# A four-unit attention and expert kernel: the last unit's jobs prepare the rows that the routed experts read

## The reference, cut to what matters

```
x = x + t0 * attention(q = norm(x), k, v = split(ctx), key bias and length mask)       # unit 0
x = x + t1 * (self-attention(norm(x)) + sum over the 2 best of 8 dense 256x256 experts) # unit 1
x = x + t2 * (attention(norm(x)) over ctx and own keys) @ w_proj.T + b_proj             # unit 2
y = norm(x)
o = causal self-attention(y) @ w_o                                                      # unit 3
h = norm(y + o) * g1 + b1
w = two best of softmax(h @ wg), scaled to sum 1
moe = sum over the two: (gelu(h @ w1[e] + bb1[e]) @ w2[e] + bb2[e]) * w[e]     # 256 -> 1024 -> 256
x = x + t3 * (norm(h + moe) * g2 + b2)
```

## Time and profile before

| | before |
|---|---|
| median of three runs | 2734.83 us (2731.59 to 2737.47) |
| the profiled execution | 2733.68 us, span 2732.0 us |
| TensorE busy | 2326.2 us |
| ScalarE, VectorE, GpSimd busy | 1381.1, 1705.4, 917.7 us |
| DMA | 296.34 MB, 108 GB/s in the mean |

### The profile page before, as it was taken

How to read it: one execution, slowest core, us unless ns; L and a number is a source line. 1 busy time by engine, 2 the same in 40 slices (tenths; PEclk the granted TensorE clock), 3 DMA queues, 4 the chain that set the end, 5 groups by cost and what they waited for, 6 DMA issues and landing times. The chain is left out here.

```text
span 2732.0 us, 52598 instructions
## 1 busy us (share of the span) xinstructions
PE 2326.2 (85%) x17492; PEld 1615.3 (59%) x17493; DVE 1705.4 (62%) x4564; ACT 1381.1 (51%) x2430; POOL 917.7 (34%) x1769
## 2 busy tenths in 40 slices
PE   3889899999999999999999999898337999999920
PEld 1445555455555555666566666665337999999920
DVE  4668796766776766766766667665455434344358
ACT  3779863454444447777777777676110222222211
POOL 5355322131232152233322257665001333333321
PEclk9989999999999999999999999999556999999965
DMA  7888633242332354454454446553560111111144
GB/s 227 215 210 209 150 97 78 51 96 55 81 82 76 94 126 117 118 122 117 113 126 118 104 110 140 133 129 76 204 189 12 35 36 36 35 35 34 36 148 167
DMA packets 214243, 296.34 MB, mean 108 GB/s; under 512 B 33109, under 2 KB 152703, under 8 KB 207776
## 3 DMA queue, kind: packets, MB, share of 16 engines
q1 hardware_dynamic: 183808, 253.78, 36.5%
q10 hardware_dynamic: 23328, 22.06, 2.6%
q0 software_dynamic: 6912, 17.97, 2.1%
HBM read 201.41 MB, written 93.22 MB: 108 GB/s over the span
## 5 line engine op out<-in xcount | busy, mean ns | idle before, releaser
L1112 DVE TENSOR_REDUCE mx<-s_ps 128x2 f32<-128x512 f32 (+1 forms) x1024 | 657.2, 683 | 217.5 <-PE s_ps L870 141.3
L995 ACT ACTIVATE ex<-t_ps 128x512 f32<-128x512 f32 (+1 forms) x1280 | 683.8, 577 | 191.7 <-PE t_ps L901 146.9
L901 PE MATMUL t_ps<-qs,ks 123*128 123x256 bf16 x2048 | 362.1, 278 | 10.3 <-ACT ex L995 6.5
L926 PE MATMUL pv_ps<-ex,va 128*32 128x256 f32 (+1 forms) x5120 | 324.7, 380 | 2.5 <-POOL ex L1035 2.5
L989 ACT ACTIVATE qs<-tr_ps 27x2048 bf16<-27x2048 bf16 x128 | 239.4, 1870 | 146.5 <-PE tr_ps L883 143.8
L847 PE MATMUL pre_ps<-wexp,xt 128*128 128x512 f32 x512 | 264.5, 625 | 6.8 <-DVE moe L1176 2.6
L1631 PEld LDWEIGHTS x_up_ps<-x_rows_t,x_wnow 128*128 128x128 f32 x2272 | 266.4, 193 | 5.3 <-issue 0.9
L1631 PE MATMUL x_up_ps<-x_rows_t,x_wnow 128*128 128x128 f32 x2272 | 267.0, 276 | 1.1 <-DVE x_pre L1694 0.7
L901 PEld LDWEIGHTS t_ps<-qs,ks 123*128 123x128 bf16 x2048 | 175.0, 99 | 143.4 <-ACT ex L995 66.2
L1641 PE MATMUL x_y_ps<-wdn,x_act 128*128 x1136 | 257.1, 379 | 0.7 <-DVE x_y L1702 0.7
L1661 ACT ACTIVATE x_rows_t<-x_rt_ps 128x256 f32<-128x256 f32 x72 | 27.7, 384 | 439.8 <-PE x_rt_ps L1620 439.8
(11 more groups left out here) (254 smaller groups left out, 3764.1 us busy)
## 6 DMA issues: line engine op xcount, KB each, us to landing
q_parts<-pq SPq DMA_DIRECT2D x128, 192.0 KB
qs<-q_parts SPq DMA_DIRECT2D x64, 384.0 KB, 5.0
qs<-q_parts SPq DMA_DIRECT2D x192, 128.0 KB, 5.8
k_parts<-pk SPq DMA_DIRECT2D x96, 192.0 KB
ks<-k_parts SPq DMA_DIRECT2D x96, 192.0 KB
ks<-k_parts SPq DMA_DIRECT2D x288, 64.0 KB
ks<-ctx_k_parts SPq DMA_DIRECT2D x64, 192.0 KB
ks<-ctx_k_parts SPq DMA_DIRECT2D x192, 64.0 KB
```

What stands on the lines that cost most here:

```text
L901: last = pe.matmul(dst[:, t * T:(t + 1) * T], key[0:ROWS, h, t * P:(t + 1) * P], qs[q_at][0:ROWS, h, :], start=True, stop=True)
L926: last = pe.matmul(pv_ps[i * VW:(i + 1) * VW, q0:T], val[:, t, k * QH + i, :], e, start=r == 0 and t == 0, stop=r == srcs - 1 and t == NT - 1,
L995: act.activation(ex[:, n % EXPS, 0:w], t_ps[n % 2][:, 0:w], ACT.Exp).then_inc(t_read, 1)
L1112: dve.tensor_reduce(dst, s_ps[n % S_BANKS][:, :].rearrange("p (a b) -> p a b", a=dst.shape[-1]), AX.X, ALU.max).then_inc(s_read, 1)
```

## The change

- The jobs of unit 3 get six more steps: `HNS` (moments of `h`, VectorE), `HNP` (root, GpSimd), `HNX` (scaling, VectorE), `HNG` (times `g1`, plus `b1`, GpSimd), `HT` (transposes and their copy by ScalarE) and `HG` (gate logits, copied by VectorE into a tile `gate_logits` that stays). The rows that they store are the normed ones. The loop of `route` is gone.
- All loads of the experts' weights stand after the attention phase: 16 halves of `wup` on ScalarE ahead of its exponential; `bup`, `bdn` and 8 of `wdn` on SyncE.
- `NX` goes from 5 to 7, `AHEAD_JOBS` from 6 to 8.
- Values are laid out 17 columns wide (`VW`) in SBUF; in PSUM the heads keep their distance of 32 (`VS`). Unit 2 loads the values' half of `ctx` from the input and GpSimd lays it out again, in place of `STOREV` and `LOADV`.
- In four jobs of unit 1 a clearing of key rows (`UNBIAS`, VectorE) is replaced by a transfer of a row of zeros (`bring_bias`).
- `JOBS` is written as a general expression of `BEHIND`; its list is the same as before. `KV_USERS`, `KEY_JOBS`, `CTX_JOBS` and `OTT_JOBS` index who used a buffer before; for this list they name the same jobs as the old expressions. `GATE` waits for the `FIN` of the job two back.

```diff
-VW = 32
+VW = HD + 1
+VS = 32
 UNITS = 4
-JOBS = [(u, b) for u in range(UNITS) for b in range(B)]
+BEHIND = (0, B, 2 * B, 3 * B)
+JOBS = [(u, n - BEHIND[u]) for n in range(B + BEHIND[-1]) for u in range(UNITS) if 0 <= n - BEHIND[u] < B]
 JOB = {job: j for j, job in enumerate(JOBS)}
 
-NX, NCTX, NPART, NQ, NKV, NO = 5, 2, 2, 3, 4, 3
+NX, NCTX, NPART, NQ, NKV, NO = 7, 2, 2, 3, 4, 3
...
+    "HNS": [("dve", 1.16)], "HNP": [("pool", 1.3)], "HNX": [("dve", 1.1)], "HNG": [("pool", 2.4)], "HT": [("pe", 0.44), ("act", 0.6)], "HG": [("pe", 0.45), ("dve", 0.2)],
...
-AHEAD_JOBS = 6
+AHEAD_JOBS = 8
 TOPS = 6
-PRE = ("XT", "KT", "Q", "K", "V", "GATE", "CT", "MBIAS", "EXPERT", "OTT", "PROJ")
+PRE = ("XT", "KT", "Q", "K", "V", "GATE", "CT", "MBIAS", "EXPERT", "OTT", "PROJ", "HT", "HG")
...
-    x = add("LOADX", 0, ("STOREX", u - 1, b, 0) if u else None, ("STOREX", *old, 0) if old else None)
+    x = add("LOADX", 0, ("STOREX", u - 1, b, 0) if u else None, (("STOREX" if old[0] < 3 else "PROJ"), *old, 0) if old else None)
...
-    if u == 0:
-        c = add("LOADC", 0, past("KT", NCTX), past("VC", NCTX))
-        values.append(add("VC", 0, c, *values_free(0), ("STOREV", 0, b - NKV, 0) if b >= NKV else None))
-        add("STOREV", 0, values[0])
-    if u == 2:
-        values.append(add("LOADV", 0, *values_free(0)))
+    if u in (0, 2):
+        before = CTX_JOBS[CTX_AT[(u, b)] - NCTX] if CTX_AT[(u, b)] >= NCTX else None
+        c = add("LOADC", 0, ("VC", *before, 0) if before else None, ("KT", *before, 0) if before and before[0] == 0 else None)
+        values.append(add("VC", 0, c, *values_free(0)))
     free = [past(n, NQ, 0, (1, 2, 3)) for n in ("K", "Q", "V")] + [past("EXPERT", NQ, (t, e), (1,)) for t in range(NT) for e in range(0, E, 2)]
-    turned = add("XT", 0, s, *free)
+        values.append(add("V", 0, turned, *values_free(srcs - 1)))
...
-    clear = add("UNBIAS", 0, *keys_free(0, 0), *keys_free(0, 1)) if u == 1 and b < NKV else None
-        chain = add("GEXP", 0, add("GATE", 0, turned))
+        chain = add("GEXP", 0, add("GATE", 0, turned, ("FIN", u, b - 2, 0) if b >= 2 else None))
...
-        add("PROJ", 0, add("OTT", 0, *outs), bp if u == 2 else None)
+        before = OTT_JOBS[OTT_AT[(u, b)] - 2] if OTT_AT[(u, b)] >= 2 else None
+        s = add("PROJ", 0, add("OTT", 0, *outs, ("PROJ", *before, 0) if before else None), bp if u == 2 else None)
+    if u == 3:
+        s = add("HNX", 0, add("HNP", 0, add("HNS", 0, s)))
+        s = add("HT", 0, add("HNG", 0, s), ("HG", u, b - 2, 0) if b >= 2 else None)
+        add("HG", 0, s)
     add("STOREX", 0, last_of(u, b))
...
+        spent = wexp[:, :, :, :].rearrange("p c e n -> p (c e n)")
+        g1, b1, wg1 = spent[:, 0:D], spent[:, D:2 * D], spent[:, 2 * D:2 * D + DC * E].rearrange("p (c e) -> p c e", c=DC)
+        ht = [spent[:, (4 + 2 * k) * D:(6 + 2 * k) * D].rearrange("p (c t) -> p c t", c=DC) for k in range(2)]
...
+                def bring_bias(u, b, src, g):
+                    at = kv_at(u, b, src)
+                    if row_dmas(at) > STACK_DMAS:
+                        sp.dma_start(ks[at % NKV][PRODUCTS:BIAS, g * HG:(g + 1) * HG, :],
+                                     bias_d[b if biased(at) else B].unsqueeze(1).broadcast_to([3, HG, T])).then_inc(k_rows[g][at % NKV], 16)
...
+                    if step == ("LOADX", 3, 0, 0):
+                        sp.wait_ge(fin_done, len(FIN_AT))
+                        sp.dma_start(g1, a["ln1_g"].partition_broadcast(P)).then_inc(norm_loaded, 16)
+                        sp.dma_start(b1, a["ln1_b"].partition_broadcast(P)).then_inc(norm_loaded, 16)
+                        sp.dma_start(wg1, a["w1_gate"].rearrange("(c p) n -> p c n", p=P)).then_inc(norm_loaded, 16)
                     if name == "LOADX":
-                        if nth_x:
...
-                        sp.dma_start(va[at][:, :, :, :].rearrange("p t h w -> p (t h w)"), vc_d[b]).then_inc(vc_loaded[b % 2], 16)
+                            before = CTX_JOBS[CTX_AT[(u, b)] - NCTX]
+                            sp.wait_ge(vc_ready, VC_AT[("VC", *before, 0)] + 1)
+                            if before[0] == 0:
+                                wait_copied(sp, ("KT", *before, 0))
+                        cols = slice(0, 2 * D) if u == 0 else slice(D, 2 * D)
+                        sp.dma_start(ctx[at][:, :, cols], tiles(ctx_in[b][:, cols])).then_inc(ctx_loaded[at], 16)
...
-                                    last = pe.matmul(pv_ps[i * VW:(i + 1) * VW, q0:T], val[:, t, k * QH + i, :], e,
+                                    last = pe.matmul(pv_ps[i * VS:i * VS + VW, q0:T], val[:, t, k * QH + i, :], e,
                                                      start=r == 0 and t == 0, stop=r == srcs - 1 and t == NT - 1,
-                                                     tile_position=(0, i * VW))
+                                                     tile_position=(0, i * VS))
...
+                    elif name == "HT":
+                        pe.wait_ge(h_scaled, HNG_AT[("HNG", u, b, 0)] + 1)
+                        end_pre(step, turn_tokens(bank, o[o_at]))
+                    elif name == "HG":
+                        pe.wait_ge(norm_loaded, 48)
+                        wait_copied(pe, ("HT", u, b, 0))
+                        end_pre(step, project(bank, wg1, ht[b % 2], E, range(NT)))
...
+                    elif name == "HNP":
+                        pool.wait_ge(h_moments, HNS_AT[("HNS", u, b, 0)] + 1)
+                        s.done(pool.tensor_scalar(hrstd[b % 2][:, :], hmv[b % 2][:, :, 1], EPS, None, ALU.add))
+                        s.wait()
+                        pool.tensor_tensor(hrstd[b % 2][:, :], hrstd[b % 2][:, :], power[:, :], ALU.pow).then_inc(h_rooted, 1)
+                    elif name == "HNG":
+                        rows = o[uses_before("o", (u, b))[1]]
+                        pool.wait_ge(norm_loaded, 48)
+                        pool.wait_ge(h_normed, HNX_AT[("HNX", u, b, 0)] + 1)
+                        s.done(pool.tensor_tensor(rows[:, :, :], rows[:, :, :], g1.unsqueeze(1).broadcast_to([P, NT, D]), ALU.mult))
+                        s.wait()
+                        pool.tensor_tensor(rows[:, :, :], rows[:, :, :], b1.unsqueeze(1).broadcast_to([P, NT, D]), ALU.add).then_inc(h_scaled, 1)
...
+                    elif name == "HNS":
+                        wait_copied(dve, ("PROJ", u, b, 0))
+                        for t in range(NT):
+                            s.done(dve.bn_stats(hstats[b % 2][:, t, :], o[o_at][:, t, :]))
+                        s.wait()
+                        for t in range(NT):
+                            last = dve.bn_aggr(hmv[b % 2][:, t, :], hstats[b % 2][:, t, :])
+                            if t < NT - 1:
+                                s.done(last)
+                        last.then_inc(h_moments, 1)
+                    elif name == "HNX":
+                        dve.wait_ge(h_rooted, HNP_AT[("HNP", u, b, 0)] + 1)
+                        for t in range(NT):
+                            last = dve.tensor_scalar(o[o_at][:, t, :], o[o_at][:, t, :], hmv[b % 2][:, t, 0:1], hrstd[b % 2][:, t:t + 1], ALU.subtract, ALU.mult)
+                            if t < NT - 1:
+                                s.done(last)
+                        last.then_inc(h_normed, 1)
+                    elif name == "HG":
+                        end_pre(step, dve.tensor_copy(gate_logits[:, b * NT:(b + 1) * NT, :], bank[:, 0:NT * E].rearrange("p (t e) -> p t e", t=NT)))
...
+                for x in range(E):
+                    for c in range(DC):
+                        act.dma_start(a["wup"][:, c, x, :], a["w_up"][x, c * P:(c + 1) * P, :]).then_inc(a["w_loaded"], 16)
 
                 act.wait_ge(lg_ready, 1)
                 act.activation(pr[:, :, :].rearrange("p a b -> p (a b)"), z8[0][:, :, :].rearrange("p a b -> p (a b)"), ACT.Exp).then_inc(lg_exp, 1)
 
...
+                sp.dma_start(a["bup"][:, :, :].rearrange("p e f -> p (e f)"), a["b_up"].rearrange("e (f p) -> p (e f)", p=P),
+                             allow_slow_non_contiguous=True).then_inc(a["w_loaded"], 16)
+                sp.dma_start(a["bdn"][:, :, :].rearrange("p e f -> p (e f)"), a["b_down"].rearrange("e f -> (e f)").partition_broadcast(P)).then_inc(a["w_loaded"], 16)
+                for x in range(E):
+                    sp.dma_start(a["wdn"][:, x, :, :], a["w_down"][x].rearrange("(f p) n -> p f n", p=P)).then_inc(a["w_loaded"], 16)
```

291 lines of the change are left out of this document (92 added, 199 removed).

## The result

The changed kernel took **2616.86 us** in the median (2609.42 to 2620.26), the kernel before 2735.26; the ratio is 0.957 (95% interval 0.954 to 0.959). I had said 2660, with a range of 2620 to 2700. The direction was right, the size was not: 118 us for 75.

What follows compares the result with a forecast made beforehand. No engine was busy all the time, TensorE nearest with 85%. Route −81.4, unit 3 +14, its open chain +6.3, unit 0 −10, units 1 and 2 −4: −75 from 2734.8, so 2660 us, range 2620 to 2700.

Steps and rivals of the forecast that it cites:

- Looking further ahead pays: Attention phase, rival: units 0 to 2 lose 30 to 45 us of gaps, about 2622 us; chance 0.11.
- W: Route after attention: time from the start of VectorE's routing chain to ScalarE's exponential, bounded between 6.4 and 57 us.
- The same work inside unit 3: a loss, +14: Unit 3's 16 jobs: added norm and logit work costs 14 us, two thirds of TensorE's 22 added.
- +6.3: Behind unit 3's last residual: the last job's norm chain stands in the open until its rows are stored, 6.3 us.
- Rival 4: Attention phase pays 25 to 50 us, GpSimd's new operations and waits standing ahead of masks; 2690 to 2715 us, chance 0.09.
- Unit 0, −10: Unit 0: sixteen value stores go and x tiles are asked for earlier; 0 to −30 us, taken as −10.
- Units 1 and 2, −4: Units 1 and 2: order changes, work does not; together −4 us, a worse interleaving given 25.
- I take W = 25: Route: exponential 25 us after chain start: about 9 behind `bup`, 6.4 own issues, some 9 held by a full queue.
- the 1.69 us row: Old loop, 1973.01: ScalarE's issue took 1.69 us, not 0.40, after SyncE's loads; read as SyncE's loads holding ScalarE.
- rival 1: Route: ScalarE issues freely, exponential 7 to 12 us after chain start; 2644 us, chance 0.17.
- The end of the loop, −102.2: After attention: the loop of norms goes, so the routing chain begins 3 us after 1922.02 instead of 105.2.
- the chain's 55.5 us: Route: from the exponential's end to the experts' first gather, 55.5 us, which stay.

## Why the prediction was wrong

**"Looking further ahead pays" was the rival nearest to what came, and its price was read in the wrong place.** I gave it 0.11 and 2622 us, and held against it that only 9.2 us of waits for x stand in unit 0. That is what VectorE waits for rows that are late, and to take it as the measure of the lookahead is the step that failed. In unit 3 this wait is 0.5 us in the changed kernel and 2.6 in the one without lookahead, and their times differ by 71. The lookahead is worth 71 us in the changed kernel and 29 without the steps of `h`, of which the prediction had at most 14 (unit 0's 10 and the 4 of units 1 and 2). By which wait it pays stays open: SyncE's for a free tile doesn't follow the time either. That the rival's 2622 lies so near is luck in part: it asked 30 to 45 us of units 0 to 2, which gave 23, and it had W at 25, which gave 14.5.

**"The same work inside unit 3: a loss, +14" was right in mechanism and size,** as far as the scatter of the orders allows: 16.7 us when taken out (12 in the windows of unit 3), and "+6.3" behind the last residual was 7.5. Unit 3 nevertheless got 6 us shorter, so the mark that I had set for it (350 to 360 long) would have called a right term wrong. GpSimd's share there was as said: 259.10 of 338 us, 77%. Rival 4, an attention phase that pays 25 to 50 us for the new steps, was no fancy either: without the lookahead they cost 46 to 62 us. What I missed is that two parts of the change act on each other: the same steps cost 20 us with lookahead.

**"Unit 0, −10" was half of it:** 21 us, of which 11 are the stores, which I had counted in MB and not priced, and 4 the lookahead; 6 are not assigned. The granted clock there rose from 0.94 to 0.99: by the estimate (1 − 0.94) × 307 = 18 us of lost clock time became 3, which would be 15 of the 21. It is not that simple: without lookahead the clock was 0.96, 12 us by the same estimate, and the unit was only 4 us longer. I had named the mechanism and taken a third of its range.

**"Units 1 and 2, −4"** was −2. It hides about −20 from the lookahead and 12 to 16 lost again; to what, isn't settled, and the order's luck is of that size.

**"I take W = 25" failed at the 1.69 us row.** This is the second step that failed, for 14 us. From one issue that took 1.69 for 0.40 us I concluded that ScalarE is held by what SyncE has put in. Two kernels say no: with 8192 pieces outstanding on SyncE's queue ScalarE issues in 0.66 us each, and with the pieces on its own it sits 25 us while SyncE goes on. W was 10.5, in the bounds and inside rival 1 (7 to 12), and the wait in it 9.7, under the 12 that I had set as the sign of being wrong. The other sign, issues of `wup` over 0.5 us, came true at 0.66 and told nothing. I named the rule of the Trainium skill (DMA: Bandwidth & Descriptors, "HWDGE ordering") beside it: one ring for SP and one for ACT on the same 16 engines. The trace agrees with that sentence (626 packets of each from 1916 to 1922), but I had drawn from it what it doesn't say, that a full ring of the one holds the issues of the other. What caused the 1.69 us is open. ScalarE's own queue had more ahead than I said (0.36 MB of earlier loads moved on it from 1970 to 1971), and from 1973 to 1974 it moved nothing while SyncE's moved 0.30 MB.

**The end of the loop, −102.2, and the chain's 55.5 us held:** the chain starts 11.9 us behind the residual's end and the gather comes 55.5 us after the exponential's end, as before. The weights were in by 1960 at the latest (0.30 of the 16 us to the gather), 55 us after the first issue; I had said 57 from the chain's start.

The sum with what the runs gave: the chain starts 11.9 us behind the residual's end for 107.8 (−95.9), the wait in W is 9.7 for 3.3 (+6.4), the steps of `h` in unit 3 cost 16.7, the stores give 10.5, the lookahead 29 where the steps of `h` don't need it. That is −112.3. The profile says −116.1. That the two meet to 4 us is luck in part: the terms of the attention phase depend on which kernels are paired, and one pair moved by 18 us with the order alone.

## What to carry to other kernels

A consumer's waits for data don't bound what more tiles and a longer horizon give: 9.2 us of such waits stood against 29 to 71 us here. Nor did the issuing engine's wait for a free tile price them; the kernels with five and seven tiles did. Added work and added slack must be priced together: measure the two-by-two, since the same steps cost 20 us in a schedule with room and 46 to 62 in one without; and change the order at random once or twice to learn how much of a difference is luck (here up to 18 us). What one queue had outstanding in small pieces held that queue's issuer and not the other's: put many-piece loads on the queue of the engine that has nothing urgent to run.
